# GpSimd clears a spare row, waited for, ahead of each row scatter of the attention stage

## The reference

```python
h = tokens(x)                                   # (64, 170, 128)
h = h + attention(layernorm(h))
xf = layernorm(h).reshape(-1, 128)              # 10880 rows
gate_vals, idx = top_k(xf @ router_w, 2)        # two of eight experts a token
gates = softmax(gate_vals)
for e in range(8):
    y = layernorm(xf + relu(xf @ w1[e] + b1[e]) @ w2[e] + b2[e]) * gamma[e] + beta[e]
    out += sum(where(idx == e, gates, 0)) * y
h = h + out
```

## Time and profile before

| | us |
|---|---|
| median of 3 runs | 1073.56 (1072.31 to 1076.19) |
| the profiled execution | 1084.83 |
| its span, first to last instruction | 1083.1 |
| attention stage, within the span | about 272 to 673 |
| expert stage and sums | about 681 to 1083 |

### The profile page before, as it was taken

How to read it: one execution, slowest core, us unless ns; L and a number is a source line. 1 busy time by engine, 2 the same in 40 slices (tenths; PEclk the granted TensorE clock), 3 DMA queues, 4 the chain that set the end, 5 groups by cost and what they waited for, 6 DMA issues and landing times.

```text
span 1083.1 us, 27789 instructions
## 1 busy us (share of the span) xinstructions
PE 880.4 (81%) x7792; PEld 728.9 (67%) x7793; DVE 761.3 (70%) x3156; ACT 582.1 (54%) x1536; POOL 448.2 (41%) x491
## 2 busy tenths in 40 slices
PE   2578989789999899999999961799999999999900
PEld 1478989756666666666667641688888888888800
DVE  2258787625776767666666663398898998899856
ACT  0344351046777767776766741466666666666600
POOL 3000000000354444444444455277777777777720
PEclk9999999957797878787866765799999999999955
DMA  6365530060111111111111112622222222222259
GB/s 133 63 98 83 73 53 2 31 188 14 35 43 43 51 41 46 41 43 41 41 41 41 41 50 79 244 73 70 71 70 67 76 67 67 69 72 70 60 222 396
DMA packets 69075, 84.10 MB, mean 78 GB/s; under 512 B 12052, under 2 KB 53703, under 8 KB 68859
## 3 DMA queue, kind: packets, MB, share of 16 engines
q1 hardware_dynamic: 54282, 54.93, 20.3%
q0 software_dynamic: 12256, 22.50, 6.7%
q10 hardware_dynamic: 2448, 5.57, 1.3%
HBM read 48.15 MB, written 35.71 MB: 77 GB/s over the span
## 4 chain that ended last, share of the span: by engine, by line
PE 61%; DVE 10%; issue 8%; ACT 6%; DMA 4%; another core or an unknown queue 2%; ACTq 1%; POOL 1%; SPq 1%; DVEq 1%; POOLq 0%
PE ps L886 8%; PE ps L651 7%; PE ps L732 5%; PE ps L877 5%; PE ps L707 4%; PE ps L875 4%; PE ps L876 3%; DMA arena<-y_tokens 3%; DVE arena L985 3%; PE ps L781 3%; PE ps L713 3%; PE ps L718 3%; PE ps L800 2%; PE ps L767 2%; PE ps L786 2%
## 5 line engine op out<-in xcount | busy, mean ns | idle before, releaser
L552 POOL DMA_INDIRECT x_slots<-arena x192 | 186.3, 970 | 268.8 <-ACT arena L1427 80.1
L1546 ACT ACTIVATE arena<-ps,b_t 128x256 f32<-128x256 f32 x368 | 156.8, 478 | 89.4 <-PE ps L877 81.8
L579 POOL DMA_INDIRECT y_tokens<-arena x184 | 185.5, 1008 | 46.6 <-issue 44.0
L886 PE MATMUL ps<-arena 128*128 x1472 | 182.1, 277 | 0.4 <-ACT arena L1546 0.4
L886 PEld LDWEIGHTS ps<-arena 128*128 128x128 f32 x1472 | 172.7, 193 | 2.5 <-issue 0.5
L651 PE MATMUL ps<-wt,arena 128*128 128x128 f32 x960 | 118.1, 280 | 14.3 <-DVE arena L985 14.3
L651 PEld LDWEIGHTS ps<-wt,arena 128*128 128x128 f32 x960 | 112.7, 195 | 16.0 <-DVE arena L985 16.0
L875 PE MATMUL ps<-arena 128*128 128x256 f16 x368 | 102.0, 277 | 23.9 <-DVE arena L1262 15.1
L1101 DVE TENSOR_TENSOR arena<-ps,cst 85x340 f32<-85x340 f32 x128 | 59.6, 502 | 65.2 <-PE ps L732 58.1
L876 PE MATMUL ps<-arena 128*128 128x256 f16 x368 | 101.5, 276 | 0.0
L877 PE MATMUL ps<-arena 128*128 128x256 f16 x368 | 101.5, 276 | 0.0
(11 more groups left out here) (204 smaller groups left out, 1848.1 us busy)
## 6 DMA issues: line engine op xcount, KB each, us to landing
arena<-x_slots SPq DMA_DIRECT2D x92, 130.0 KB
arena<-y_tokens SPq DMA_DIRECT2D x17, 640.0 KB, 14.3
h<-h_rows SPq DMA_DIRECT2D x1, 5440.0 KB, 16.5
out<-h ACTq DMA_DIRECT2D x17, 320.0 KB, 9.4
arena<-x_in SPq DMA_DIRECT2D x64, 84.5 KB
arena<-x_in SPq DMA_DIRECT2D x64, 78.0 KB
h_rows<-h SPq DMA_DIRECT2D x32, 128.0 KB
x_slots<-arena POOLq DMA_INDIRECT x192
```

Source lines behind the costliest of these rows:

```text
L552: pool.indirect_dma_start(xs_dram, bass.IndirectOffsetOnAxis(ap=slot_i[n][0:rows, t, k:k + 1], axis=0), row[n][0:rows, k, t, :], None).the ...
L579: pool.indirect_dma_start(y_dram, bass.IndirectOffsetOnAxis(ap=y_id[n % 2][:, k:k + 1], axis=0), y_sl[n % 2][:, k, :], None, bounds_check= ...
L886: ins = pe.matmul(ps[6 + m][:, 128 * k:128 * k + 128], hid[m][:, c, 128 * k:128 * k + 128], w2_sb[:, bass.ds(e, 1), c, :].rearrange("p o n ...
L1546: act.activation(hid[m][:, c, :], ps[2 + 2 * m + c // 2][:, SLOT * (c % 2):SLOT * (c % 2) + SLOT], ACT.Relu, bias=b1_t[:, bass.ds(e * FC + ...
```

## The change

GpSimd gets a memset of one partition by 512 float32 words, at the end of the arena that holds the stage's tiles, ahead of each of the 192 scatters. It signals a new semaphore, and GpSimd waits for that signal before the scatter. The waits on VectorE's steps stay and come first. Nothing else reads or writes the spare row.

```diff
+SPACER = 512
...
+        spacer = arena[0:1, ARENA_WORDS - SPACER:ARENA_WORDS]
...
                         elif (t, k) == (2, 1):
                             after("gate_done", p + 1)
+                        pool.memset(spacer, 0.0).then_inc(S["spaced"], 1)
+                        pool.wait_ge(S["spaced"], 2 * (PTILES * p + t) + k + 1)
                         pool.indirect_dma_start(
                             xs_dram, bass.IndirectOffsetOnAxis(ap=slot_i[n][0:rows, t, k:k + 1], axis=0),
                             row[n][0:rows, k, t, :], None).then_inc(scattered[n], 16)
```

More of the change, by code:

```diff
@@ L290, in build @@
         hid.append(A3.take(FC, SLOT))
+        assert A3.at <= ARENA_WORDS - SPACER
         A3.at = 0
@@ L319, in build @@
             "yl4 yl5 yl6 yl7 sum_ready rstd0_done nb_done xmn_done xhn_done tr_full tr_free y_full "
-            "h_added dch ach pch t_prep d_prep xen_done "
+            "spaced h_added dch ach pch t_prep d_prep xen_done "
         ).split()
```

## The result

The changed kernel takes 1033.2 us (median, 1028.69 to 1046.91) where the kernel before takes 1074.88 beside it on the same chip: ratio 0.957 with a 95% interval of 0.951 to 0.963, so 4.3% faster.

The account below looks back on a forecast made before the run. TensorE was taken to bound the attention stage, and GpSimd's scatters its end. Tail +10.1, stalls -2 and VectorE +1 gave +9.1 us on 1073.56: 1082.7 us, range 1069 to 1092.

Parts of the forecast that it names:

- What bounds the kernel: TensorE sets the pace of the attention stage, busy 341 of 371 us; in the 38 us after it, GpSimd's scatters do.
- One memset and its cycle: On GpSimd, a memset of 519 ns plus gaps makes one scatter's cycle 1.91 us, with ends of 1.63 and 2.08.
- Does GpSimd become the bound: Six scatter cycles take 11.5 us against a pair's 12.8 us, so GpSimd keeps up on the mean in the attention stage.
- The tail: From 624.09 us on GpSimd's scatters end 11.8 us later, 1.7 of it hidden: a cost of 10.1 us.
- Inside the stage: TensorE's 21.2 us of stalls in `outputs` shift with the scatters' places: a gain of 2 us, ends -12 and +10.
- the nine new stalls: Nine clear phases of `outputs` get a scatter 0.33 us into them, at about 1 us each: a loss of 9.
- VectorE beside the memset: The memset may hold up small VectorE instructions in the attention stage: 1 us, 0 to 5.
- A: Rival: memsets part close scatters, stalls in `outputs` go, none come, cycle near its lower end; -8.3, 1065 us, chance 0.12.
- C: Rival: cycle 2.08 us, scatters nearly always inside `outputs`; 1097 us, chance 0.10; decided where six scatters fill a pair's 12.8 us.
- The signs named ahead: Profile: 192 memsets of 0.52 us, GpSimd busy 100 us more, SyncE waiting 10 us for scatters, fewer long `outputs` stalls.

Follow-up runs that it names:

- e13: The changed kernel with a memset of 256 words in place of 512, on a quiet chip: 967.3 us, ratio 1.007 to the kernel before.
- e11: The kernel before without the scatters' waits on VectorE's steps, and without memsets, on a stalling chip: 1127.4 us, ratio 1.050 to the kernel before.
- e18: The changed kernel with a memset of 384 words in place of 512, on a stalling chip: 1008.6 us, ratio 0.936 to the kernel before.
- e9: The changed kernel with a memset of 128 words in place of 512, on a stalling chip: 1052.8 us, ratio 0.985 to the kernel before.

## Why the prediction was wrong, point by point

**What bounds the kernel: right, half read.** TensorE set the pace. The prediction quoted the clock of 0.78 with the busy time and never asked what it was worth. This is where the gain lay. It also put the 11.3 us by which the profiled execution was longer down to profiling. Other runs don't bear that out: the profiled execution is the shortest of its ten in e13 (953.2 us) and the longest of four in the changed kernel, so this was the spread between executions.

**One memset and its cycle: right.** 515 to 516 ns against 519 (the row with 128 partitions gave the time of one with a single partition: 256 words took 302 ns in e13, 305 in the earlier trace rows). The Trainium skill (GPSIMD Engine Reference, Instruction dispatch) says that all eight cores get the instruction and that it is complete when all are done; it gives no time for fewer partitions, and the run, with no discount, agrees with it. The gap to the scatter was 0.28 to 0.30 us for 0.28. The gap ahead was nothing, for 0.15, so the cycle is 1.77 us for 1.91.

**Does GpSimd become the bound: wrong by its divisor.** The step set six cycles against the 12.8 us that a pair took before. Those 12.8 were made of the stalls and the clock behind them. Without them TensorE needs 9.4, and six cycles of 1.77 are 10.6. GpSimd is then late early in the stage, not from 624 us on. The end of the stage, changed kernel: GpSimd's last scatter, and SyncE's queue as it starts the loads that waited for it.

```profile
637.93 0.93 POOL L557 DMA_INDIRECT x_slots<-arena  x1 [0.30 <-POOL arena L555]
```

```profile
641.09 3.84 SPq L432 DMA_DIRECT2D arena<-x_slots  x4
```

**The tail: right mechanism, too small.** The pause of GpSimd went and SyncE's queue waits 10.6 us for the last scatters (from 629.6 to 640.2) where it waited 0.8, as forecast. But the tail costs +16.7 us (20.0 - 3.3) and not +10.1. The cycle was shorter than forecast, so this isn't its size: TensorE's part was 65 us shorter, and GpSimd, which can't follow, was left with more behind it. (The sum also has one cycle too many: the scatter at 624.09 us is the 162nd, so 30 follow it. With its own 1.91 us the term would have been 8.2.)

**Inside the stage: the step that failed.** The forecast was -2 us, with ends of -12 and +10, and TensorE's part of the stage gave -65. Two errors. First, the cause was read from positions alone: a scatter 0 to 1.5 us into the phase stalls it. The positions did fit 28 phases, but so did another reading, which the prediction noted in passing for seven of them: the stalls come with two scatters close together. All 15 stalled phases of the kernel before have a pair 1.24 to 1.32 us apart, and the sixteenth, which the positions didn't explain (0.4 us), has one too. Clear phases have such pairs as well, but there the second scatter starts 0.7 us or more ahead of the phase or 2.9 us or more into it or behind it: in this trace it takes the pair and the place. The changed kernel has a scatter 0.04 to 0.52 us into nine phases and no stall in them, so the nine new stalls (a loss of 9 us) never came. Second, and larger: a stall was priced at its own length, 21.2 us at the most. Those went, and 65 us came back. Behind the sixth `outputs` the idle time fell by 15 us, and 49 us are the same 2992 matmuls done faster, because less of the time passed at the 1.2 GHz level (clock 0.79 before, 0.93 after).

**VectorE beside the memset: right, no weight.** VectorE's groups with three elements, changed kernel, 290 to 640 us (busy us, mean ns):

```profile
L1194 DVE TENSOR_SCALAR arena<-arena 128x3 f32<-128x3 f32 x31 | 7.4, 238 | 0.0
...
L1178 DVE TENSOR_SCALAR arena<-arena 128x3 f32<-128x3 f32 x31 | 6.4, 205 | 0.0
```

They took 211 and 158 ns: 31 times 0.03 and 0.05 us, beside a stage that is 65 us shorter. The copy of the same shape went from 159 to 206 ns; a reciprocal and an operation on two tensors of it stayed (171 and 170 ns, 155 and 158). The Trainium skill (SBUF — State Buffer, Who interferes with whom) has a VectorE copy, cast or tensor_scalar in a two-port mode wait for a GpSimd instruction that came first. Which of the rows grew agrees with it; in which mode they ran, no row shows.

**Rivals.** A, that the spacing pays, is what happened, with a chance of 0.12 and 1065 us. Its mechanism is right in each word but the last, since the cycle is 1.77 us and its lower end was 1.63: the pairs part, the stalls go, no new ones come. Its price had the same fault, 12 us for the stalls of 21, and it put the tail at 3.7 us where it cost 16.7. C's point of decision, six scatters that fill a pair, was reached as well, at a lower cycle than forecast, since the pair had shrunk. On a quiet chip it is all that happens: 4.4% slower.

**The signs named ahead.** The memset row, the 192 times, the 100 us more of GpSimd and SyncE's 10 us all came. "The forecast is wrong if TensorE's waits at lines 760 and 767 fall below 5 us" came too.

## What stays open

What blocks TensorE isn't shown. The trace calls the idle time "issue" or "remote", and no row names a holder; that it goes with the distance of scatters is shown by the kernels of the table above, on chips of one kind only, and e11 shows that it isn't the distance alone. No run spaces the scatters by waiting without a memset, so whether GpSimd's work between them matters beside the time is untested. Why two kinds of chips run the same kernel in 965 and 1075 us isn't known either, nor whether it is the chip at all or something of the moment, such as what else ran on it. (One chip was met twice and was the same both times.) What makes up the remaining two thirds of the 25 us in the expert stage is open too. 256 words cost 0.7% on a quiet chip; that kernel met no stalling one, so whether it would be the best for both is not known. e18 is the best measured on the stalling kind; 128 words cost nothing on the other and gain 1.5% on this one.

## What to carry to other kernels

Where the granted clock sits between its two levels in a stage that TensorE bounds, price each stall with the clock that follows it, not with its own length; a run of small products that stands still for a microsecond with no named releaser is worth more than its microseconds. When a queue is to have more work, set its capacity against the pace that the bound engine would have without its stalls, and find the smallest dose: here 384 words beat 512 on the one kind of chip and cost half as much on the other. And a gain that lies in stalls with no named cause has to be measured on a second chip.

## What the runs showed of the hardware

GpSimd's indirect scatters of 128 rows, started 1.27 to 1.45 us apart, go with gaps of 0.3 to 2.1 us in TensorE's small products, fp32 in `outputs` and bf16 at lines 804 and 806. At 1.66 us `outputs` holds 1.2 us of gaps, and elsewhere gaps of up to 0.65 us with no releaser remain (10.3 us of 250 in e18); at 1.77 us there are 1.8 and 0.9 us. This holds on one kind of chip; on the other 1.27 us apart does nothing.

A memset in one partition took 102, 196, 302, 409 and 516 ns for 16, 128, 256, 384 and 512 words: a straight line of 0.83 ns a word from about 90 ns. A signal of GpSimd to itself and the start of a scatter behind it take 0.28 to 0.30 us.

TensorE idled 12 us of 200 in pieces of up to 0.6 us with its clock at 1.00 (e18), and lost half its clock behind pauses of 1.2 us followed by two or three smaller ones (e9, e11). In the kernel before, where a pause of 0.5 us and one of 1.3 us came within two us of each other, 7 us at half clock followed.
